# ScalarE's order inside a block of a scan kernel: silu and tanh in one visit, quarters of delta moved, weight loads of the last block spread

## What is computed

```python
C_t = tanh(proj[..., N:]); B_t = softplus(proj[..., :N])      # first layer, N = 64
y   = first_scan(u, B_t, C_t) @ Wo + bo
xn  = layernorm(y) * g + b;  x_br, z = split(xn @ W_in)       # Mamba, 1024 channels
xb  = silu(causal_conv(x_br))
delta = softplus(xb @ W_delta + b_delta)                      # 1024 x 1024 weight
h_t = exp(delta_t * A) * h_(t-1) + delta_t * B_t * xb_t       # 16 states for each channel
out = ((h_t * C_t).sum() + xb * D) * silu(z) @ W_out + y
x   = x + out                                                 # then:
x   = x + ffn(x + x @ (base + low_rank(cond)))                # rows of the low-rank factor from c2_w2
```

## Time and profile before

| | |
|---|---|
| median of 3 runs | 2678.2 us (2674.68 to 2682.89) |
| the profiled execution: time, span | 2683.99 us, 2681.9 us |
| mean granted TensorE clock | 0.948 |
| busy, share of the span | PE 86%, DVE 84%, ACT 62%, POOL 64% |
| scans (L853) | 512, from 118.9 us to 2157.2 us |
| one block in the middle | 126.2 us |

### The profile page before, as it was taken

The page is one execution under the profiler, slowest core; times in us unless marked ns, Lnnn a source line. Parts: engine busy times, 40 slices in busy tenths (PEclk is TensorE's granted clock), DMA queues, the critical chain, the costliest instruction groups (busy, mean ns, idle before and its releaser), DMA issues. The chain is left out here.

```text
span 2681.9 us, 34173 instructions
## 1 busy us (share of the span) xinstructions
PE 2307.7 (86%) x11488; PEld 1590.2 (59%) x11520; DVE 2265.7 (84%) x2232; ACT 1665.4 (62%) x3332; POOL 1725.8 (64%) x2042
## 2 busy tenths in 40 slices
PE   7878888889898988888988888898986884999997
PEld 5656666666666665766666666666664332444443
DVE  2299999999999999999999999999997735888886
ACT  2566676666667676667676767667674434555554
POOL 0287777878787877878787878787876521232221
PEclk8889999999999999999999999999997987999999
DMA  4102020202011110202020202010114421112110
GB/s 184 72 1 71 9 74 7 75 11 74 17 63 45 36 64 17 72 10 71 9 71 9 75 5 79 17 63 25 48 57 178 175 100 55 60 59 66 63 52 24
DMA packets 47435, 151.74 MB, mean 57 GB/s; under 512 B 7973, under 2 KB 8869, under 8 KB 44206
## 3 DMA queue, kind: packets, MB, share of 16 engines
q1 hardware_dynamic: 47278, 149.76, 15.8%
HBM read 132.37 MB, written 17.37 MB: 56 GB/s over the span
## 5 line engine op out<-in xcount | busy, mean ns | idle before, releaser
L469 POOL TENSOR_TENSOR ring<-ring,Cbc 128x512 f32<-128x512 f32 x1024 | 1281.8, 1273 | 44.6 <-POOL carry L462 0.4
L853 DVE TENSOR_TENSOR_SCAN ring<-a_ps,ring 128x1024 f32<-128x1024 f32 x512 | 1168.0, 2282 | 99.3 <-ACT a_ps L691 97.9
L691 ACT ACTIVATE a_ps<-delta,nA 128x255 f32<-128x255 f32 x2048 | 850.0, 466 | 382.2 <-DVE ring L853 381.0
L1056 PE MATMUL yT_ps<-ident,ring 128*128 128x128 f32 x4096 | 586.0, 284 | 171.2 <-POOL ring L469 168.7
L845 DVE TENSOR_TENSOR ring<-u_ps,Bbc 128x1024 f32<-128x1024 f32 x512 | 619.7, 1210 | 38.1 <-PE yT_ps L1056 31.3
L1056 PEld LDWEIGHTS yT_ps<-ident,ring 128*128 128x128 f32 x4096 | 474.1, 144 | 287.9 <-POOL ring L469 245.6
L1022 PE MATMUL work<-xb,big 128*128 128x256 f32 x2048 | 474.5, 383 | 11.1 <-ACT zs L557 11.1
L1022 PEld LDWEIGHTS work<-xb,big 128*128 128x128 f32 x2048 | 384.4, 192 | 80.1 <-issue 17.8
L462 POOL TENSOR_TENSOR carry<-ring,half 128x4 f32<-128x4 f32 x512 | 126.0, 246 | 380.4 <-DVE ring L853 378.8
L1038 PE MATMUL work<-Wout,xb 128*128 128x512 f32 x512 | 242.1, 608 | 0.0
L995 PE MATMUL work<-y0s,big 128*128 128x256 f32 x1024 | 235.1, 380 | 0.7 <-issue 0.7
(11 more groups left out here) (198 smaller groups left out, 2538.9 us busy)
## 6 DMA issues: line engine op xcount, KB each, us to landing
Bbc<-bc_rows SPq DMA_DIRECT2D x64, 512.0 KB, 4.6
Cbc<-bc_rows SPq DMA_DIRECT2D x64, 512.0 KB, 3.7
xT<-in_xT SPq DMA_DIRECT2D x16, 514.0 KB, 3.6
x_rows<-x2row SPq DMA_DIRECT2D x32, 256.0 KB, 2.0
xp<-x_rows SPq DMA_DIRECT2D x32, 256.0 KB, 2.7
xx<-in_x SPq DMA_DIRECT2D x32, 256.0 KB, 3.0
out_rows<-orow SPq DMA_DIRECT2D x32, 256.0 KB, 2.0
delta<-in_c_w SPq DMA_DIRECT2D x6, 1024.0 KB, 5.1
```

Of the source, the lines that this page charges most:

```text
L469: nc.gpsimd.tensor_tensor(hp, hp, Cbc[:, G * g + GP * c:G * g + GP * c + GP, :], ALU.mult)\
L691: r = nc.scalar.activation(a_ps[q % 2][:, i, 1:T], delta[:, par, dt, 1:T], ACT.Exp, scale=nA[:, dt, s:s + 1])
L853: dve.tensor_tensor_scan(ring[:, q % RING, :, :].rearrange("p g t -> p (g t)"), a_ps[q % 2][:, :, :].rearrange("p g t -> p (g t)"), ring[: ...
L1056: r = pe.matmul(yT_ps[:, tt, :], ring[:, q % RING, i, P * tt:P * tt + P], ident[:, :], is_transpose=True, start=False, stop=(g == NG - 1 a ...
```

## The change

Of ScalarE's order in a block, it moves:

- `prj` (now exp alone) from slot 5 to slot 3; the tanh becomes `prj_tanh` in slot 4;
- `zsilu` from slot 30 to slot 4 of the following block, right ahead of that tanh, with one table load ahead of the two and one behind; `prj_ln` in slot 6 loads none any more;
- `dexp(0)` from slot 25 to 24, `dexp(1)` from 27 (behind `zcopy(2)`) to 26, `dexp(3)` from 2 to 1; `dexp(2)` stays in 31; `dln(0)` from 28 to 27, now ahead of `zcopy(3)`.

In the last block the load of `f_w2` moves up to the block's start, and 7/8 of `f_w1`, one load before, becomes seven loads of 512 KB, each behind a chunk. TensorE, DVE and POOL execute the same instructions in the same order as before.

```diff
+                    sp.wait_ge(full[BANK["DL3"]], jobs_before("DL3", k - 1) + 1)
+                    sp.dma_start(big[1][:, :], f_w2).then_inc(s_big[1], 16)
...
-                    sp.wait_ge(full[BANK["WOUT1"]], jobs_before("WOUT1", k) + 1)
-                    sp.dma_start(big[0][:, 0:7 * DI], f_w1[:, 0:7 * DI]).then_inc(s_big[0], 16)
-                    sp.dma_start(big[1][:, :], f_w2).then_inc(s_big[1], 16)
...
                         sp.dma_start(chunk[(c + 1) % 3], c2_w2[c]).then_inc(s_chunk[c % 3], 16)
+                        if 2 <= c < 9:
+                            sp.dma_start(big[0][:, DI * (c - 2):DI * (c - 1)], f_w1[:, DI * (c - 2):DI * (c - 1)])\
+                                .then_inc(s_big[0], 16)
...
+                def prj_tanh():
+                    ps = take("PRJ")
                     wait(act, s_c0, 6 * n)
                     nc.scalar.activation(c0[:, :], ps[N0:P, 0:T], ACT.Tanh, bias=sc0[N0:P, 4:5]).then_inc(s_tanh, 1)
                 def prj_ln():
-                    nc.scalar.preload_act_table_set("natural_log_exp_and_others")
...
-                next_plan = {5: [prj], 6: [prj_ln], 8: [lambda: stats(0)], 9: [lambda: stats(1)], 10: [y0scale],
+                next_plan = {3: [prj], 6: [prj_ln], 8: [lambda: stats(0)], 9: [lambda: stats(1)], 10: [y0scale],
...
+                    if q == 4 and (front or scan):
+                        nc.scalar.preload_act_table_set("silu_and_others")
+                        if scan:
+                            zsilu()
+                        if front:
+                            prj_tanh()
+                        nc.scalar.preload_act_table_set("natural_log_exp_and_others")
```

More of the change, by code:

```diff
@@ L578, in zsilu @@
                     for j in (2, 3):
-                        act.wait_ge(free[BANK[f"Z{j}"]], jobs_before(f"Z{j}", k) + 1)
+                        act.wait_ge(free[BANK[f"Z{j}"]], jobs_before(f"Z{j}", k - 1) + 1)
                     for tt in range(NT):
-                        v = zs[:, fp, tt, :]
+                        v = zs[:, par, tt, :]
                         r = nc.scalar.activation(v, v, ACT.Silu)
@@ L641, in rowcopy @@
                     nc.scalar.activation(xw[:, c % 2, :], work[0][0:2, :], ACT.Copy).then_inc(s_rowcp, 1)
-                next_plan = {5: [prj], 6: [prj_ln], 8: [lambda: stats(0)], 9: [lambda: stats(1)], 10: [y0scale],
+                next_plan = {3: [prj], 6: [prj_ln], 8: [lambda: stats(0)], 9: [lambda: stats(1)], 10: [y0scale],
                              11: [y0back], 14: [lambda: xcopy(0)], 15: [lambda: xcopy(1)], 16: [lambda: xcopy(2)],
                              17: [lambda: xcopy(3), silu], 20: [bc], 21: [lambda: zcopy(0)], 23: [lambda: zcopy(1)],
[L647 to L650, removed]
+                             24: [lambda: dexp(0, False)], 26: [lambda: dexp(1, False)],
+                             27: [lambda: zcopy(2), lambda: dtail(0, False), lambda: dln(0, False)],
+                             28: [lambda: zcopy(3)], 31: [lambda: dexp(2, False)]}
+                scan_plan = {1: [lambda: dexp(3, True)], 2: [lambda: dtail(1, True)], 6: [lambda: dln(1, True)]}
                 turned = {13: 0, 20: 1, 28: 2}
@@ L1217, in _ @@
                 for i, q in enumerate((q1, q2)):
-                    act.wait_ge(s_big[i], 32 if i == 0 else 16)
+                    act.wait_ge(s_big[i], 16 * (F * KD // DI) if i == 0 else 16)
                     nc.scalar.activation(q[:, :, :].rearrange("p a b -> p (a b)"), big[i][:, :], ACT.Abs,
```

## The result

The changed kernel takes 2716.49 us (median; 2715.75 to 2720.62), the one before 2677.98 beside it: ratio **1.0145**, 95% interval 1.0127 to 1.0164. It is slower, and 3.5 us above the forecast of 2713. Source lines have moved: the scan is L866, a(q) L704, a quarter of delta L605 and L607, DVE's input of a slot L858, the factor row L1111.

The account below looks back on a forecast made before the run. DVE was taken as the bound (118.0 of 126.2 us busy). First block 4.5, 14 rounds x 3.6 = 50, 1.5 into the last block, less 21: +35 on 2683.99, 2719, or 2713 at the median; likeliest case 2698 to 2727, range 2674 to 2728.

Parts of the forecast that it names:

- Slot 26, the stall of 2.2 us: Scan 26 waits a new 2.2 us for a(26), behind `dexp(1)` waiting for TensorE's DL1; s(27) comes 1.85 later.
- DL2 as what is late next: Slot 31: `dexp(2)` waits for TensorE's DL2, so of 4.62 us taken from ScalarE only 0.3 reach DVE.
- `dexp(3)` ahead of a(1) costs nothing: Slot 1: a(1), behind `dexp(3)` waiting for DL3, is still ready 1.6 us before scan 1 needs it.
- The 1.5 us at slot 0: Scan 0 of the next block comes 1.5 us late, by the same amount as scan 31.
- What DVE does between two scans keeps its time: Assumption of the walk round the block: DVE's work between scans is unchanged, so sections give only lateness.
- The visit of slot 4, +2.1 us: From s(0) to y0: scan 4 stalls 2.3 us, and y0 ends 2.1 us later.
- The first block, +4.5 us: a(1) waits for DL3 there, so scan 4 comes 2.9 to 5.2 us late; 4.5 taken.
- The last block, -21: The chunk for row 1 lands sooner, saving 21 of DVE's 22.56 us wait for TensorE (18 to 25).
- Only one of the two stalls is real: Rival: without slot 26's stall 2671 us, without slot 4's 2674; chance 0.12.
- Faster: Rival: ScalarE absorbs the moves, both stalls go, 2629 us; chance 0.07.
- The loads collide again: Rival: in the last block chunks are still late and the gain of 21 falls away, 2734 us; chance 0.06.
- The drain is paid: Rival: at 2.66 us per table switch the visit is 2.8 longer ahead of scan 4, 2754 us; chance 0.01.

Follow-up runs that it names:

- quarter1_back: The changed kernel with only `dexp(1)` moved back, from slot 26 to the head of slot 27, ahead of `zcopy(2)`: 2692.88 us (ratio 1.0046).
- dma_alone: The kernel before with the new weight loads of the last block alone, ScalarE's order as before: 2657.03 us (ratio 0.9932).
- exp_behind: The changed kernel with PRJ's exp moved from slot 3 to slot 4, behind the visit's second table load: 2684.62 us (ratio 1.0023).
- both_back: The changed kernel with the edits of quarters_back and exp_behind at once: 2646.74 us (ratio 0.9873).
- visit_back: The changed kernel with silu back in slot 30 and exp, tanh and load back in their old places, quarters as changed: 2668.24 us (ratio 0.9956).
- quarters_back: The changed kernel with `dexp(0)`, `dexp(1)`, `dln(0)` and `dexp(3)` back in their old slots, visit of slot 4 kept: 2685.46 us (ratio 1.0028).
- order_alone: The changed kernel with the old weight loads in the last block, so ScalarE's new order alone: 2734.07 us (ratio 1.0210).
- silu_preload: dma_alone with slot 17's table load for silu asked for ahead of `xcopy(3)`: 2641.72 us (ratio 0.9861).

## Why the prediction was right

- **Slot 26, the stall of 2.2 us**: 2.16 us, in nearly every round; quarter1_back shows the cause. s(27) came 1.74 us late (2.16 + 0.49 - 0.91), forecast 1.85.
- **DL2 as what is late next**: right. From s(27) to s(31) are 14.25 us, forecast 5.70 + 5.3 + 0.04 + 1.43 + 1.72 = 14.19; the releaser is TensorE, and scan 31 waits 1.69 (forecast 1.6). Of the 4.62 us of ScalarE taken out of slot 30 hardly any reached DVE.
- **`dexp(3)` ahead of a(1) costs nothing**: right; scan 1 does not wait.
- **The 1.5 us at slot 0**: the term was mis-sized. "What DVE does between two scans keeps its time" failed at one instruction, the `u_ps` above, and from s(31) to s(0) are 5.76 us in place of 6.67. s(31) was 1.74 - (14.56 - 14.25) = 1.4 late, s(0) only 0.5.
- **The visit of slot 4, +2.1 us**: the stall is 2.77 (forecast 2.3), and `y0` starts 21.64 us after s(0), against 19.12: +2.5. PRJ, full 7.78 us after s(0) before, is now full 8.33 after it, since TensorE did not come sooner with DVE; so 0.55 of what DVE had won ahead of slot 0 came back here. From `y0` on I had changed nothing and put the term at nothing; 0.4 was lost there at one input that waits 0.75 us for TensorE, 0.35 in dma_alone, while the clock in the 10 us from 15 us behind s(0) is 0.57 against 0.83 before. 0.5 + 2.5 + 0.4 and 0.1 over the rest: a round is 3.5 us longer, forecast 3.6. Three terms were off by up to 1 us, and that they cancel to 0.1 is luck.
- **The first block, +4.5 us**: +0.2 between the two profiled executions, and yet the mechanism was right. The kernel before took 17.12 us for 64 matmuls there; the changed one took 14.08, and so did seven of the nine others (exp_behind 17.04, both_back 15.47). Against dma_alone, which has the same order as before, scan 4 comes 5.4 us later: 134.04 against 128.64. Of that 4.1 lie behind s(0), where scan 1 waits 3.31 us and scan 4 1.50; 1.3 lie ahead of s(0) already, which the forecast did not have.
- **The last block, -21**: -18.9 in the last round, which holds the lateness at s(0) too, 0.6 as measured: -19.5, against 22.56 - 2.88 = 19.7 at DVE's one long wait. The chunk for row 1, issued at 2105.82, lands after 5.4 us, 0.9 ahead of the row's matmuls, and the sevenths delay no row: none of the later ones waits for a chunk.
- **The rivals.** "Only one of the two stalls is real" falls with the two waits, each of which a repair takes away by itself. The prices that I gave it were 2674 without the stall of slot 4 (visit_back has 2668, exp_behind 2685) and 2671 without that of slot 26 (quarters_back: 2685. Its scan 31 comes 0.3 us sooner than before and not 1.3, for TensorE's chain, but `u_ps` gives 0.9 back; what the price lacks is 0.4 of the visit's stall and the lost 1.1 us of every second round.) "Faster" fails by the same rows. "The loads collide again" fails by row 1, whose matmuls wait 1.25 us and not 18.45; its price, 2734, is what order_alone measures with the old loads. "The drain is paid": the visit with tanh is 1167.20 - 1162.09 = 5.11 us, forecast 4.99; the two loads, two silus and the tanh of the rows are 1.28 + 2.01 + 0.47 + 1.28 = 5.04 of it, which leaves no room for 2 x 1.38. The drain of 1380 ns that the Trainium skill states (ScalarE: Activation LUTs, section "What ACT_TABLE_LOAD costs") is not seen in any kernel here.
- **The level**: the sum of +35 was against the profiled execution, and the 0.2% down to the median made 2713 of 2719. The median came at 2716.5, since the spans lie 32 us apart but the medians 38; the fall of the clock in the first block of that one execution (some 5 us, below) would explain it. The forecast's own range was added up a little too wide: 4.5 + 59 + 1.5 - 18 above the median is 2725, not 2727.

## What to carry to other kernels

Do not let an engine that works in program order wait for a job of another engine ahead of an operation that a third one needs: moving work "earlier" by one slot put two waits for TensorE (5.36 and 2.75 us of ScalarE) in front of decays whose inputs were ready. Before a move, compare when its input is full with when the instruction behind it is needed; a table load was worth placing ahead of such a wait (1.28 us at scan 17), since it waited for nothing. The costs of two moves need not add, where both bring the same saving elsewhere (`u_ps`, 0.93 us); here the gains of the two repairs did add, which only the run with both could show.

## What the runs showed of the hardware

The granted clock at the same matmuls differs between profiled executions whose work up to there has the same order. First the kernel before, then dma_alone, timeline of TensorE:

```profile
105.51 17.12 PE L1022 MATMUL work<-xb,big 128*128 128x256 f32 x64 [1.76 <-ACT zs L557]
```

```profile
103.37 14.08 PE L1025 MATMUL work<-xb,big 128*128 128x256 f32 x64 [1.77 <-ACT zs L560]
```

and the windows over 100 to 125 us of the same two (the column ahead of the last two is the granted clock):

```profile
100.00:125.00 25.00, 22.55 (x85) 17.92 (x85) 9.39 (x11) 16.29 (x30) 7.65 (x11) 0.86 0.10 41
```

```profile
100.00:125.00 25.00, 22.66 (x108) 18.42 (x108) 13.78 (x14) 20.47 (x41) 11.08 (x15) 1.00 0.03 8
```

The idle time ahead was the same (1.76 and 1.77 us), the clock 0.86 and 1.00 of full speed in the mean, the lower with stretches at half (0.50 from 105 to 110 us), which is 1.2 in place of 2.4 GHz. The first scan 17 comes some 5 us later with it, 186.8 against 181.6. The changed kernel and exp_behind, which differ in the place of one exp, are nearly such a pair: with the same 1.39 us of idling ahead the 64 matmuls take 14.08 us at a clock of 1.00 and 17.04 at 0.86, and scan 0 starts at 115.0 and 118.0. In the first 60 us of the last block the clock goes from 0.80 (silu_preload) to 0.89 (dma_alone), and the last round of the kernels with spread loads from 130.9 to 126.7. Executions of one kernel spread over 14 us (dma_alone, 2653.6 to 2667.7) or only 3 (exp_behind). So a difference of 5 us between two single executions need not come from the edit, while the means of the middle rounds agree to 0.1 us where ScalarE's order is the same (126.1 twice, 129.6 twice).
